# Second attention: activations, gathers, combines and stores of rows moved to other chunks of the pipeline

## The reference

```python
y = _layer_norm(x, ln1_w, ln1_b)
q = jnp.tanh(einsum(y, W_Q)) * (PI / 4);  k = jnp.tanh(einsum(y, W_K)) * (PI / 4)
V = jnp.einsum('btd,idh->btih', y, W_V)
heads = cos(q) * cumsum(cos(k) * V) + sin(q) * cumsum(sin(k) * V)
denom = cos(q) * cumsum(cos(k)) + sin(q) * cumsum(sin(k)) + COS_EPS
x = x + jnp.einsum('dhi,btih->btd', W_O, heads / denom)
y = _layer_norm(x, ln2_w, ln2_b)
x = x + jnp.dot(jax.nn.gelu(jnp.dot(y, W1) + b1), W2) + b2
```

## Time and profile before

| | us |
|---|---|
| median of 3 runs | 2822.84 (2822.49 to 2823.51) |
| the profiled execution's own time | 2810.92 |
| its span, first to last instruction | 2808.9 |
| PE busy in the span | 2444.4 (87%) |
| DVE busy | 1828.7 (65%) |
| ACT busy | 1343.2 (48%) |
| POOL busy | 814.7 (29%) |

### The profile page before, as it was taken

The page is one execution under the profiler, slowest core; times in us unless marked ns, Lnnn a source line. Parts: engine busy times, 40 slices in busy tenths (PEclk is TensorE's granted clock), DMA queues, the critical chain, the costliest instruction groups (busy, mean ns, idle before and its releaser), DMA issues. The chain is left out here.

```text
span 2808.9 us, 53468 instructions
## 1 busy us (share of the span) xinstructions
PE 2444.4 (87%) x20412; PEld 2173.2 (77%) x20412; DVE 1828.7 (65%) x3234; ACT 1343.2 (48%) x2053; POOL 814.7 (29%) x1194
## 2 busy tenths in 40 slices
PE   4999999952899999745777888869999999999999
PEld 3666666631899999624666777769999999999999
DVE  7666666663688888679888878457454454544544
ACT  1555555620577777432334443434554545545454
POOL 4556666237000000145666655510000000000000
PEclk7999999975899999867899999989999999999999
DMA  9994000003677777556555455235222222232222
GB/s 300 330 329 152 2 2 2 2 29 124 201 234 231 240 230 236 166 155 155 130 144 134 133 130 139 59 121 158 93 80 97 85 91 85 80 97 86 91 78 87
DMA packets 194350, 373.31 MB, mean 133 GB/s; under 512 B 28708, under 2 KB 104680, under 8 KB 193128
## 3 DMA queue, kind: packets, MB, share of 16 engines
q1 hardware_dynamic: 184792, 343.31, 40.5%
q0 software_dynamic: 9360, 27.27, 2.8%
HBM read 336.95 MB, written 100.66 MB: 156 GB/s over the span
## 5 line engine op out<-in xcount | busy, mean ns | idle before, releaser
L2300 DVE TENSOR_TENSOR e_h_lo<-e_h,e_h_hi 128x512 fp32r<-128x512 f32 x320 | 222.1, 694 | 300.7 <-ACT e_h_hi L2376 300.7
L2438 PE MATMUL e_h_ps<-e_yT_hi,e_w_hi 128*128 128x256 f32 x1280 | 362.5, 283 | 3.0 <-ACT e_h L2362 2.2
L2454 PE MATMUL e_y_ps<-e_w_hi,e_h_hi 128*128 128x256 f32 x1280 | 358.9, 280 | 2.3 <-DVE e_h_lo L2300 2.2
L2438 PE MATMUL e_h_ps<-e_yT_lo,e_w_hi 128*128 128x256 f32 x1280 | 358.4, 280 | 0.0
L2438 PE MATMUL e_h_ps<-e_yT_hi,e_w_lo 128*128 128x256 f32 x1280 | 358.3, 280 | 0.0
L2454 PE MATMUL e_y_ps<-e_w_hi,e_h_lo 128*128 128x256 f32 x1280 | 355.4, 278 | 0.0
L2454 PE MATMUL e_y_ps<-e_w_lo,e_h_hi 128*128 128x256 f32 x1280 | 355.3, 278 | 0.0
L2376 ACT ACTIVATE e_h_hi<-e_h 128x512 fp32r<-128x512 f32 x320 | 202.2, 632 | 277.2 <-DVE e_h L2295 220.9
L2362 ACT ACTIVATE e_h<-e_h_ps,e_b 128x512 f32<-128x512 f32 x320 | 218.8, 684 | 174.9 <-PE e_h_ps L2438 152.6
L2295 DVE TENSOR_TENSOR e_h<-e_h,e_spread 128x512 f32<-128x512 f32 x256 | 176.9, 691 | 133.3 <-ACT e_h L2362 132.2
L462 DVE TENSOR_REDUCE a_top<-a_ring 128x2 f32<-128x1024 f32 (+3 forms) x256 | 204.2, 819 | 71.5 <-PE a_ring L651 70.0
(11 more groups left out here) (364 smaller groups left out, 6835.8 us busy)
## 6 DMA issues: line engine op xcount, KB each, us to landing
e_w<-in_w SPq DMA_DIRECT2D x78, 1024.0 KB, 5.8
e_spread<-share_store SPq DMA_DIRECT2D x512, 128.0 KB, 2.9
a_keys<-rows_store SPq DMA_DIRECT2D x128, 256.0 KB, 4.9
a_queries<-rows_store SPq DMA_DIRECT2D x86, 256.0 KB, 5.0
a_running_hidden<-rows_store SPq DMA_DIRECT2D x42, 256.0 KB, 4.9
e_xs<-sorted_x SPq DMA_DIRECT2D x39, 256.0 KB, 5.0
sorted_y<-e_ys POOLq DMA_DIRECT2D x39, 256.0 KB, 6.0
e_stage_buf<-in_w_all SPq DMA_DIRECT2D x10, 512.0 KB, 4.2
```

The source lines that it names most:

```text
L2300: dve.tensor_tensor(h_parts[q % 2][1][:, :], h[:, q % 2, :], h_parts[q % 2][0][:, :], ALU.subtract).then_inc(h_lo.sem, h_lo.tick())
L2438: last = pe.matmul(h_ps[q % 2][:, cols], l, r, start=(m == 0), stop=(m == len(ops) - 1))
L2454: last = pe.matmul(y_ps[n][:, 0:D], h_parts[q % 2][a][:, n * P:(n + 1) * P], w2[b][:, c, :], start=(q == 0 and m == 0), stop=(q == CH - 1 ...
```

## The change

Nothing is computed differently; instructions move. On ACT the two tanh go ahead of the copy of the heads in c 2, and the sine goes to the end of c 3, behind `back_channel`. On POOL `refine_front` goes from c 1 to c 3, and the gathers of the four tiles go one by one into c 4, 5, 6 and 7 (before: two in c 4, two in c 5). On DVE `combine` LEFT goes from c 6 to c 7, RIGHT from c 7 to c 0 of the next block, `spread_of` from c 0 to c 2, `centre_of` from c 3 to c 5. On SP `store_rows` becomes `store_keys` (in c 5, as soon as the sine is done) and `store_queries` (in c 6, behind `spread_keys`).

```diff
--- before.py
+++ after.py
@@ -1433,12 +1433,16 @@
                     sp.wait_ge(combined.sem, combined.at(2 * TB, 0))
                 sp.dma_start(raw(m, c, n), t[name].rearrange("(c p) n -> p c n", p=P)).then_inc(staged[STAGED[m][0]].sem, 16)
 
-            def store_rows(s, m):
+            def store_keys(s, m):
+                sp.wait_ge(trig_ready.sem, trig_ready.at(1, s))
+                for j in range(2):
+                    sp.dma_start(rows_store[m, j], trig[j * QUAD:j * QUAD + H1, 1, :]).then_inc(rows_stored.sem, 16)
+                sp.wait_ge(rows_stored.sem, rows_stored.at(32, s))
+
+            def store_queries(s, m):
                 sp.wait_ge(rows_ready.sem, rows_ready.at(1, s))
                 for j in range(2):
-                    rows = slice(j * QUAD, j * QUAD + H1)
-                    sp.dma_start(rows_store[m, j], trig[rows, 1, :]).then_inc(rows_stored.sem, rows_stored.tick(16))
-                    sp.dma_start(rows_store[m, 2 + j], den[rows, :]).then_inc(rows_stored.sem, rows_stored.tick(16))
+                    sp.dma_start(rows_store[m, 2 + j], den[j * QUAD:j * QUAD + H1, :]).then_inc(rows_stored.sem, 16)
                 sp.wait_ge(rows_stored.sem, rows_stored.at(64, s))
 
             def spread_keys(n):
@@ -1458,18 +1462,21 @@
                 sp.dma_start(t["x3"][s:s + 1, :, :, :].rearrange("o p n d -> p (o n) d"),
                              g.x[:, s * TB:(s + 1) * TB, :]).then_inc(loaded.sem, loaded.tick(16))
 
-            store_rows(0, 0)
+            store_keys(0, 0)
+            for c in range(KEYS):
+                spread_keys(c)
+            store_queries(0, 0)
             for c in range(QUERIES):
-                if c < KEYS:
-                    spread_keys(c)
                 spread_queries(c)
             for n in range(STAGES):
                 s, c = n // HC, n % HC
-                if c == 6 and live(s + 1):
-                    store_rows(s + 1, (s + 1) % 2)
+                if c == 5 and live(s + 1):
+                    store_keys(s + 1, (s + 1) % 2)
                 if n + KEYS < CHUNKS:
                     sp.wait_ge(weighted_ready.sem, weighted_ready.at(2 * (n + 1)))
                     spread_keys(n + KEYS)
+                if c == 6 and live(s + 1):
+                    store_queries(s + 1, (s + 1) % 2)
 
                 for at in (() if c == 5 else (n - 1, n) if c == 6 else (n,)):
                     if at + QUERIES < CHUNKS:
@@ -1539,14 +1546,12 @@
                                        ALU.subtract).then_inc(heads_lo.sem, heads_lo.tick())
                 if c == 1 and live(s - 1):
                     refine(s - 1)
-                if c == 1 and s >= 1 and live(s + 2):
-                    refine_front(s + 2)
                 if c == 2 and live(s - 1):
                     residual(s - 1)
-                if c == 4 and live(s + 3):
-                    gather(s + 3, range(2))
-                if c == 5 and live(s + 3):
-                    gather(s + 3, range(2, TB))
+                if c == 3 and s >= 1 and live(s + 2):
+                    refine_front(s + 2)
+                if c >= 4 and live(s + 3):
+                    gather(s + 3, range(c - 4, c - 3))
 
         @block.vector
         def _(dve):
@@ -1741,6 +1746,8 @@
                 if n in (2, 4):
                     low_weights(3 if n == 2 else 4)
                 if c == 0 and s >= 1 and live(s + 2):
+                    combine(s + 2, RIGHT)
+                if c == 2 and s >= 1 and live(s + 2):
                     spread_of(s + 2)
                 if c == 1 and live(s + 1):
                     front(s + 1, m, "low0")
@@ -1753,12 +1760,10 @@
                     back(s - 1, "norm")
                 if c == 4 and live(s + 1):
                     front(s + 1, m, "keys")
-                if c == 3 and s >= 1 and live(s + 2):
+                if c == 5 and s >= 1 and live(s + 2):
                     centre_of(s + 2)
-                if c == 6 and live(s + 3):
+                if c == 7 and live(s + 3):
                     combine(s + 3, LEFT)
-                if c == 7 and live(s + 3):
-                    combine(s + 3, RIGHT)
 
         @block.scalar
         def _(act):
@@ -1799,6 +1804,7 @@
                     for q in range(2):
                         act.wait_ge(angles.sem, angles.at(q + 1, s))
                         act.activation(trig[:, q, :], h_ps[0:ROWS, :], ACT.Tanh).then_inc(tanhs.sem, tanhs.tick())
+                if at == "sines":
                     act.wait_ge(tanhs.sem, tanhs.at(2, s))
                     act.activation(trig[:, :, :], trig[:, :, :], ACT.Sin, scale=float(np.pi / 4),
                                    bias=phase[0:ROWS, :]).then_inc(trig_ready.sem, trig_ready.tick())
@@ -1828,6 +1834,7 @@
             front(0, 0, "turn1")
             high_weights(1)
             front(0, 0, "angles")
+            front(0, 0, "sines")
             norm_front(1)
             front(0, 0, "denominator")
             high_weights(2)
@@ -1836,6 +1843,8 @@
                 s, c, done, u = n // HC, n % HC, n - 1, n - BACK
                 if 0 <= u < CHUNKS:
                     hidden_chunk(u)
+                if c == 2 and live(s + 1):
+                    front(s + 1, (s + 1) % 2, "angles")
                 if 0 <= done < CHUNKS:
                     act.wait_ge(heads_ready.sem, heads_ready.at(done + 1))
                     if done == 0:
@@ -1846,13 +1855,13 @@
                             heads_hi.tick())
                 if c == 0 and live(s + 1):
                     front(s + 1, (s + 1) % 2, "turn1")
-                if c == 2 and live(s + 1):
-                    front(s + 1, (s + 1) % 2, "angles")
                 if c == 2 and live(s - 1):
                     norm_back(s - 1)
                 if c == 3 and live(s - 1):
                     back_channel(s - 1, 0)
                     back_channel(s - 1, 1)
+                if c == 3 and live(s + 1):
+                    front(s + 1, (s + 1) % 2, "sines")
                 if c == 5 and live(s + 1):
                     front(s + 1, (s + 1) % 2, "denominator")
                 if c == 6 and live(s + 2):
```

## The result

The changed kernel takes 2782.86 us (median of 4 runs, 2774.21 to 2794.43) where the kernel before took 2822.66 in the same session: 39.8 us less, a ratio of 0.9859, with a 95% interval of 0.9819 to 0.9899. It is faster, by 1.4%. Two of the four runs lie at 2774 and two at 2791 and 2794. The prediction was 2775 us (2757 to 2806), 47.7 us less.

What follows compares the result with a forecast made beforehand. DVE's work plus its waits, 78.9 us over the second attention, were taken to bound the kernel. Gains of 67.7 us less losses of 18 and 2 left 47.7, so 2822.84 became 2775 us, range 2757 to 2806.

Steps and rivals of the forecast that it cites:

- Items 1 and 2: Early tanh and refine_front in c 3 remove DVE's waits for V, 18.2 us; those for the heads go, 18.7 us.
- Item 3: Sine out of the path to the transposes, and earlier tanh: DVE's waits for the transposes go, 20.8 us.
- Item 4: DVE's waits for keys at first chunk and c 0 of blocks 6, 7: 10.0 of 20.1 us gone.
- Item 5: DVE in c 4: new waits for the heads' sum and the sine, 3.0 us in six blocks, 18 us lost.
- Item 6: combine on DVE: LEFT at 4.2, RIGHT at 3.3 us, 2 us lost over five blocks; bounds 3 gain, 25 loss.
- Item 7: Moving spread_of and centre_of on DVE, and store_keys' waits on SP, cost nothing; the number of table loads stays.
- The rival on `combine`: POOL's tensor operations slow both halves on DVE, costing 25 us and not 2: 2798 us; chance 0.09.
- The one on new waits: Rival: new waits in the layer's chain over five streams eat most of the gain, 2790 to 2817 us; chance 0.17.
- PE's gap ahead of the second angles product: Sign: in the changed trace PE stands below 1 us before that product, where it stood 4.87 us.
- blocks 1 to 4: Sign: these blocks of the second attention run at 66 to 67 us in the changed trace.
- PE's granted clock: Sign of being wrong: the clock granted to PE falls in c 1 to c 3.

Runs made afterwards that it cites:

- the last kernel: Changed kernel with gathers paired, LEFT in c 6, and SP sending c 1's queries and the token store behind c 1's keys: 2733.59 us, ratio 0.9715.

## Why the prediction was right, point by point

*Items 1 and 2, V and the heads.* 18.2 and 18.7 us were forecast; 19.3 - 1.0 = 18.3 and all 18.7 went. The sizes hold. The share of the edits was otherwise than drawn: `refine_front` in c 3 brought 14.7 of the 18.3 alone, and with the rest of the change in place the tanh was not needed for V. Undoing it costs 15 us all the same, half or more of it in short DVE instructions that then meet POOL, which the prediction did not have in view.

*Item 3, the transposes.* 20.8 forecast, 20.8 gone. The reason given, 2.44 us of the sine and 4.8 of the tanh together, was more than was needed: the undone sine left them at 1.3 us and the undone tanh at 2.1, so either is enough once `refine_front` is out of the way.

*Item 4, keys.* 10.0 forecast. With the queries and hidden rows, 20.1 became 8.0 + 2.3 + 0.7 = 11.0, 9.1 less, and in the places named: the two that stay are c 1 of blocks 6 and 7. But undoing the part costs 22 us. In the kernel before, by the prediction, the slow RIGHT half of `combine` ahead of c 0 hid the lateness in the early blocks; in the changed kernel RIGHT stands behind c 0, and with the late store DVE stands at the start of every block. The price of a part read from the kernel before is not its price in the kernel after.

*Item 5, "c 4 becomes the tight place".* This term was mis-sized: 18 us forecast, 4.7 measured, all for the sine, 0.9 to 1.2 us in five blocks; there was no wait for the heads in c 4.

*Item 6, `combine`.* +2 forecast; `x<-a_mixed` measured -8.2, below the bound of -3: in block 4 RIGHT, at 1505.87, found POOL idle (from 1503.7 to 1509.07), and LEFT, at 1564.60, found it at the gather of 1565.08 to 1567.3. What was missing is on the other side: tile 3 is gathered in c 7 and wanted in c 0, and that is 10.7 us of waits in four blocks. Half by half the term was wrong, and only the sum, +2.5, looks right.

*Item 7, "At no cost: `spread_of` and `centre_of` are moved on the same engine".* This is the step that failed. They are the same instructions on the same engine, but in another company. `a_centre` and `a_minus` grew by 12.3 us and `a_var` of `spread_of` by 3.6; `a_den`, which did not move itself, grew by 3.9 where POOL's operations came to it. I had put such slowing to `combine` alone, in the rival, and it came to the smallest instructions. The rule of the Trainium skill quoted there ("SBUF — State Buffer", "Who interferes with whom") is on instructions with two SBUF inputs, as `a_minus` has. With this, the trace agrees in that the long `a_minus` (4.36 us) lies over three tensor operations of POOL and its twin (0.14 us) over none, while why it didn't end before the first of them stays open. `a_var`, with one input, is not of the kind that was quoted, and took 1.32 us beside POOL's operation on the hidden. That POOL's operations in c 5 come back to back is what the spread gathers do: with pairs, `a_centre` and `a_minus` take 3.0 us and not 16.9. It takes the late sine as well: with the sine undone and the gathers spread they take 2.4, and `a_den` is the long one.

Added up: -18.3 - 18.7 - 20.8 - 9.1 + 4.7 - 8.2 + 10.7 + 19.8 is -39.9 us; `a_backT_lo`, no longer beside POOL as much, gives another 4.1, which makes 44.0 of the 43.9. Forecast 47.7. That the total was near is in part luck: errors of 13 us in item 5, of 10 in item 6 and these 4 stood against the 30 us that item 7 and the gathered rows brought. The rival on `combine` did not occur. The one on new waits did in another place: 15 us of them, two thirds for gathered rows, and not at c 4. Of the signs, PE's gap ahead of the second angles product is gone (that product now follows the matmuls of the heads at once, at 1524.23), and blocks 1 to 4 take 66.6 us in the mean, as forecast. PE's granted clock in block 4 rose from 0.91 to 0.95. In c 1 it fell from 0.85 to 0.77, which the prediction had called a sign of being wrong; it stayed at 1.00 in c 2 and rose from 0.82 to 1.00 in c 3, and no wait of DVE for PE came of it in that block.

Open: why two of the first four runs took 2792 and not 2774 (no profile is of that level), why a small DVE instruction that begins 0.6 us ahead of POOL's operations ends only with them, and what releases the 9.1 us of waits in the kernel with the old stores. And not tried: the last kernel with the sine undone as well.

## What to carry to other kernels

A short instruction on DVE is not free to move: look at what POOL does at its new place and right behind it, since the three instructions of 4.4 us all began just before a run of its tensor operations. Where several engines work in step, undo each part of a bundle by itself after it has won: here one part was worth 22 us, one 15, one nothing, and one cost 13; and two parts can cure the same wait, so that neither is missed when it alone is undone. The bundle without the one that cost and with a better order of DMAs gives twice the gain. Before moving work away from where it covers a late transfer, find the transfer: `combine` in c 0 hid the keys of c 1, and moved to c 1 it gave 12 us of waits back.

## What was not expected of the hardware

A DVE instruction on 128x4 numbers lasted 4.36 us, over three tensor operations of POOL in a row (1.29, 1.29 and 1.25 us), and did not end at a seam between them. In the kernel with `centre_of` between the halves, DVE's timeline at one `front` "queries" reads

```profile
1417.93 3.33 DVE L1638 RECIPROCAL a_den<-a_den 48x512 f32<-48x512 f32 x1
1421.30 2.32 DVE L1640 TENSOR_TENSOR a_den<-a_trig,a_den 48x512 f32<-48x512 f32 x1
```

with POOL at three tensor operations from 1419.27 to 1423.06: the reciprocal, with one input, keeps the 3.33 us that it has elsewhere, and the multiplication behind it, which takes 0.68 in block 4 of the change, takes 2.32. And rows gathered by an indirect DMA that was issued at 1498.22 were there only at 1505.87, 7.7 us later.
